# Lambda layer block on one core: the q parts are kept by chunk in DRAM and loaded in three pieces per chunk

## What is computed

```python
h = relu(bn(conv1x1(x, conv1_w)))                       # 512 -> 128 channels, x group-normed before
q = bn(conv1x1(h, q_w)); k = conv1x1(h, k_w); v = bn(conv1x1(h, v_w))   # 64, 16, 32 channels
pos = position_lambdas(emb, v)                          # 15x15 convolution, one per key
content_lambda = einsum('bkm,bvm->bkv', softmax(k), v)
out = einsum('bhkn,bkv->bhvn', q, content_lambda) + einsum('bhkn,bkvn->bhvn', q, pos)
h = bn(conv1x1(relu(bn(out)), conv3_w))                 # 128 -> 512
y = x + relu(h + residual)                              # residual: the group-normed x
```

## Time and profile before

| | us |
|---|---|
| median of 3 runs | 5737.59 |
| lowest and highest | 5727.03, 5744.17 |
| the profiled execution, its own time | 5744.49 |
| its span, first to last instruction | 5742.8 |
| PE busy in it | 4814.6 (84%) |
| DVE, ACT, POOL busy | 3049.6, 2281.4, 1042.7 |
| time of the DMA packets, share of 16 engines | 63.8% |

### The profile page before, as it was taken

How to read it: one execution, slowest core, us unless ns; L and a number is a source line. 1 busy time by engine, 2 the same in 40 slices (tenths; PEclk the granted TensorE clock), 3 DMA queues, 4 the chain that set the end, 5 groups by cost and what they waited for, 6 DMA issues and landing times.

```text
span 5742.8 us, 121523 instructions
## 1 busy us (share of the span) xinstructions
PE 4814.6 (84%) x49366; PEld 2811.5 (49%) x49366; DVE 3049.6 (53%) x4727; ACT 2281.4 (40%) x2753; POOL 1042.7 (18%) x561
## 2 busy tenths in 40 slices
PE   4888888888888888888888988888888888888887
PEld 2555455544455544554444545445554455454454
DVE  3456455565554554555555546545455454564554
ACT  1434344344343343443434433434434344343443
POOL 0012221112211122211222111221112221122212
PEclk8888889888998888998888988889988899888998
DMA  3567755667656677556675566765667755677556
GB/s 104 187 213 231 256 176 201 201 226 256 209 189 206 215 249 250 172 202 207 228 257 189 193 202 222 255 217 180 211 208 248 243 175 196 215 231 255 181 202 222
DMA packets 540275, 1217.58 MB, mean 212 GB/s; under 512 B 54312, under 2 KB 236588, under 8 KB 539820
## 3 DMA queue, kind: packets, MB, share of 16 engines
q1 hardware_dynamic: 539820, 1210.21, 63.8%
HBM read 777.68 MB, written 365.22 MB: 199 GB/s over the span
## 4 chain that ended last, share of the span: by engine, by line
PE 57%; SPq 11%; issue 10%; DVE 9%; DMA 8%; ACT 3%; POOL 1%; DVEq 0%; ACTq 0%; POOLq 0%
PE ring L524 16%; PE ring L505 13%; PE ring L649 11%; PE ring L580 6%; DMA q_parts<-region 6%; SPq L351 5%; PE ring L604 4%; DVE region L693 3%; PE ring L531 3%; DVE st L861 2%; SPq L358 2%; PE ring L536 2%; PE ring L614 2%; DMA Qt<-q_parts 1%; SPq L361 1%
## 5 line engine op out<-in xcount | busy, mean ns | idle before, releaser
L693 ACT COPY region<-ring 126x1024 f32<-126x1024 f32 x1024 | 1014.9, 1014 | 1660.8 <-PE ring L505 1645.8
L505 PE MATMUL ring<-Qt,Ep 96*126 96x256 bf16 x5120 | 862.7, 312 | 453.6 <-issue 293.7
L580 PE MATMUL ring<-h,w3T 128*128 128x512 f32 x2048 | 1067.8, 664 | 131.7 <-DVE S L1008 116.4
L693 DVE COPY region<-ring 126x1024 f32<-126x1024 f32 x512 | 623.6, 1218 | 939.7 <-PE ring L505 933.7
L524 PE MATMUL ring<-X,w1e 128*128 128x512 f32 x2048 | 971.3, 630 | 128.5 <-DVE w1e L885 128.5
L505 PEld LDWEIGHTS ring<-Qt,Ep 96*126 96x126 bf16 x5120 | 641.0, 154 | 743.7 <-issue 620.5
L1164 POOL TENSOR_TENSOR X<-X,S 128x1024 f32<-128x1024 f32 x320 | 750.3, 2349 | 1142.6 <-ACT S L732 1142.6
L649 PE MATMUL ring<-region,V 126*32 126x128 f32 x24576 | 872.1, 287 | 13.2 <-DVE region L693 12.8
L649 PEld LDWEIGHTS ring<-region,V 126*32 126x32 f32 x24576 | 667.1, 114 | 138.7 <-issue 129.4
L524 PEld LDWEIGHTS ring<-X,w1e 128*128 128x128 f32 x2048 | 408.0, 202 | 630.8 <-issue 627.5
L580 PEld LDWEIGHTS ring<-h,w3T 128*128 128x128 f32 x2048 | 407.4, 213 | 550.3 <-issue 376.7
(11 more groups left out here) (126 smaller groups left out, 3076.8 us busy)
## 6 DMA issues: line engine op xcount, KB each, us to landing
X<-x_dram SPq DMA_DIRECT2D x256, 2048.0 KB, 11.8
out_dram<-X SPq DMA_DIRECT2D x512, 512.0 KB, 6.7
Qt<-q_parts SPq DMA_DIRECT2D x768, 128.0 KB, 2.8
V<-v_windows SPq DMA_DIRECT2D x96, 1024.0 KB, 10.8
h<-S SPq DMA_DIRECT2D x1024, 64.0 KB, 2.0
q_parts<-region SPq DMA_DIRECT2D x128, 256.0 KB, 4.6
v_windows<-region SPq DMA_DIRECT2D x64, 512.0 KB, 6.2
V<-v_windows SPq DMA_DIRECT2D x32, 672.0 KB
```

The costliest lines, as they stand in the source:

```text
L505: last = nc.tensor.matmul(dst[0:TROWS, i * 256:(i + 1) * 256], taps(u, xo, yo), Q[:, :, xo * BLK + yo, :], start=(i % 2 == 0), stop=True, ...
L580: last = nc.tensor.matmul(dst[:, yb * HALF:(yb + 1) * HALF], w3T[:, t, :], src, start=True, stop=True)
L693: return engine_copy(dst, src)
```

## The change

The DRAM tensor is ordered by chunk: (chunk, part, key, head x pixel), so that a key's four heads of one chunk are one row of 8 KB. A store is now one DMA for each part: 64 partitions of 2 KB each into a target of 4 heads x 16 keys x 2 KB. A load is three DMAs, one for each part: part 0 is read three times over (a stride of 0 in front) into 48 partitions, part 1 twice into 32, part 2 once into 16, in rows of 8 KB. Partition g*16 + k of `Qt` now holds key k of product g, and its columns are ordered (chunk, head) instead of (head, chunk); the views of `Qt`, of the weights and the rest rows in `region` and of the setup's tables follow. The mask, which was written by two DMAs, takes six of 16 partitions.

```diff
-        qD = nc.dram_tensor("q_parts", (QC, NPART, N), BF16, kind="Internal").ap()
+        qD = nc.dram_tensor("q_parts", (NCH, NPART, DK, HEADS * CHUNK), BF16, kind="Internal").ap()
...
-        Qg = Qt[0:KG, :].rearrange("p (h c n b) -> p h c n b", h=HEADS, c=NCH, n=PIX)
+        Qg = Qt[0:KG, :].rearrange("p (c h n b) -> p c h n b", c=NCH, h=HEADS, n=PIX)
...
-        Wt = region[:, :].rearrange("p (u h b n) -> p u h b n", u=2, h=HEADS, b=64)
+        Wt = region[:, :].rearrange("p (u c h b n) -> p u c h b n", u=2, c=NCH, h=HEADS, b=16)
...
-                sp.dma_start(qD[:, 0, cols], q0[:, cols]).then_inc(q_out[j], 16)
-                sp.dma_start(qD[:, 1:NPART, cols], q12[:, :, cols]).then_inc(q_out[j], 16)
+                for a, src in ((0, q0[:, cols]), (1, q12[:, 0, cols]), (2, q12[:, 1, cols])):
+                    sp.dma_start(qD[j, a].rearrange("k (h n) -> h k n", h=HEADS), src).then_inc(q_out[j], 16)
 
             def load_q(im, j):
-                sp.wait_ge(q_out[j], im * 32 + 32)
-                for g, (a, _e) in enumerate(SPLIT):
-                    dst = bass.AP(Qt, g * (HEADS * N) + j * CHUNK, [[NG * HEADS * N, DK], [N, HEADS], [1, CHUNK]])
-                    sp.dma_start(dst, qD[:, a, j * CHUNK:(j + 1) * CHUNK].rearrange("(h k) n -> k h n", k=DK))\
-                        .then_inc(q_in[j], 16)
+
+                sp.wait_ge(q_out[j], im * 48 + 48)
+                n = HEADS * CHUNK
+                for a, g0, g1 in ((0, 0, 3), (1, 3, 5), (2, 5, 6)):
+                    src = bass.AP(qD.tensor, (j * NPART + a) * DK * n, [[0, g1 - g0], [n, DK], [1, n]])
+                    sp.dma_start(Qt[g0 * DK:g1 * DK, j * n:(j + 1) * n], src).then_inc(q_in[j], 16)
...
-            for i in range(2):
-                sp.dma_start(mask[:, i:i + 1], six[:, i, :]).then_inc(setup_mask, 16)
+            for g in range(NG):
+                sp.dma_start(mask[g * DK:(g + 1) * DK, :], six[:, g, :]).then_inc(setup_mask, 16)
...
-                        pe.wait_ge(q_in[j], im * (16 * NG) + 16 * NG)
+                        pe.wait_ge(q_in[j], im * (16 * NPART) + 16 * NPART)
...
-                                         Qg[:, :, c, half * 32:half * 32 + 32, 4 * k:4 * k + 4]
+                                         Qg[:, c, :, half * 32:half * 32 + 32, 4 * k:4 * k + 4]
```

More of the change, by code:

```diff
@@ L162, in lambda_block @@
         CLp = sb("CLp", [KG, DV], BF16)
-        qD = nc.dram_tensor("q_parts", (QC, NPART, N), BF16, kind="Internal").ap()
+        qD = nc.dram_tensor("q_parts", (NCH, NPART, DK, HEADS * CHUNK), BF16, kind="Internal").ap()
         vD = nc.dram_tensor("v_windows", (WPAD, WROWS, ROW), F32, kind="Internal").ap()
         vR = nc.dram_tensor("v_rest", (WPAD, ROW), F32, kind="Internal").ap()
-        Q = Qt[0:KG, :].rearrange("p (hc n b) -> p hc n b", hc=HEADS * NCH, n=PIX)
-        Qg = Qt[0:KG, :].rearrange("p (h c n b) -> p h c n b", h=HEADS, c=NCH, n=PIX)
+        Q = Qt[0:KG, :].rearrange("p (ch n b) -> p ch n b", ch=NCH * HEADS, n=PIX)
+        Qg = Qt[0:KG, :].rearrange("p (c h n b) -> p c h n b", c=NCH, h=HEADS, n=PIX)
         low = Qt[96:96 + WCOLS, :].bitcast(F32)
         Vrem = low[:, 0:NXB * ROW].rearrange("p (xb r) -> p xb r", xb=NXB)
-        Wrem = low[:, 2048:4096].rearrange("p (u h b n) -> p u h b n", u=2, h=HEADS, b=64)
+        Wrem = low[:, 2048:4096].rearrange("p (u c h b n) -> p u c h b n", u=2, c=NCH, h=HEADS, b=16)
         rep = low[0:DK, 4096:4096 + KG]
         clS = low[0:DK, 4096 + KG:4096 + KG + DV]
-        Wt = region[:, :].rearrange("p (u h b n) -> p u h b n", u=2, h=HEADS, b=64)
+        Wt = region[:, :].rearrange("p (u c h b n) -> p u c h b n", u=2, c=NCH, h=HEADS, b=16)
         T = S[:, :, :].rearrange("p h n -> p (h n)").rearrange("p (i n) -> p i n", i=2)
@@ L192, in lambda_block @@
         ident = region[:, o:o + P]; o += P
-        rep0 = region[0:DK, o:o + KG].rearrange("k (a g) -> k a g", g=NG); o += KG
-        six = region[0:DK, o:o + 2 * NG].rearrange("k (i g) -> k i g", g=NG); o += 2 * NG
+        rep0 = region[0:DK, o:o + KG].rearrange("k (g a) -> k g a", g=NG); o += KG
+        six = region[0:DK, o:o + 2 * NG].rearrange("k (g i) -> k g i", g=NG); o += 2 * NG
         RR = R * R
@@ L403, in _ @@
             sp.dma_start(wkvr[DV:KV, :], wk).then_inc(setup_in, 16)
-            emb_at = o - 2 * 128 - 2 * RR
             for g in range(NG):
-                dst = bass.AP(region, g * 16384 + emb_at, [[NG * 16384, DK], [1, RR]])
-                sp.dma_start(dst, emb.rearrange("k a b -> k (a b)")).then_inc(setup_in, 16)
+                sp.dma_start(emb6[g * DK:(g + 1) * DK, :], emb.rearrange("k a b -> k (a b)")).then_inc(setup_in, 16)
             sp.wait_ge(setup_pool, 1)
@@ L614, in rest @@
                         nc.tensor.matmul(dst.rearrange("p (h x y) -> p h x y", h=HEADS, x=4)[:, :, :, BLK - 1],
-                                         Vrem[:, xb, yb * DV:(yb + 1) * DV], Wrem[:, half, :, c * 16 + g, :],
+                                         Vrem[:, xb, yb * DV:(yb + 1) * DV], Wrem[:, half, c, :, g, :],
                                          start=False, stop=False, skip_group_check=True)
@@ L650, in lam @@
                                                         V[0:TROWS, VSLOT[t], xb, yb * DV:(yb + 1) * DV],
-                                                        Wt[0:TROWS, u % 2, :, c * 16 + g, :],
+                                                        Wt[0:TROWS, u % 2, c, :, g, :],
                                                         start=False, stop=(u % 3 == 2), skip_group_check=True)
@@ L691, in move_weights @@
             src = ring[at][0:TROWS, :].rearrange("p (n hb) -> p hb n", n=4)
-            dst = Wt[0:TROWS, u % 2, :, :, 4 * s:4 * s + 4].rearrange("p h b n -> p (h b) n")
+            dst = Wt[0:TROWS, u % 2, :, :, :, 4 * s:4 * s + 4].rearrange("p c h b n -> p (c h b) n")
             return engine_copy(dst, src)
@@ L696, in move_rest @@
             src = ring[at][96:96 + WCOLS, :].rearrange("p (n hb) -> p hb n", n=4)
-            return engine_copy(Wrem[:, half, :, :, :].rearrange("p h b n -> p (h b) n"), src)
+            return engine_copy(Wrem[:, half, :, :, :, :].rearrange("p c h b n -> p (c h b) n"), src)
         def move_sums(engine_copy, k):
@@ L1066, in _ @@
             dve.wait_ge(setup_pool, 5)
-            chain(nc.vector.tensor_copy(rep, rep0.rearrange("k a g -> k (a g)")))
-            dve.wait_ge(setup_mask, 32)
+            chain(nc.vector.tensor_copy(rep, rep0.rearrange("k g a -> k (g a)")))
+            dve.wait_ge(setup_mask, 16 * NG)
             chain(nc.vector.tensor_copy(ehi, emb6))
@@ L1126, in _ @@
                         pool.wait_ge(setup_gp, n)
-                        nc.gpsimd.memset(six[:, i, gg:gg + 1], -1.0).then_inc(setup_gp, 1)
+                        nc.gpsimd.memset(six[:, gg, i:i + 1], -1.0).then_inc(setup_gp, 1)
                         n += 1
@@ L1132, in _ @@
             nc.gpsimd.affine_select(out=rep0, in_=rep0, compare_op=ALU.not_equal, fill=1.0, base=0,
-                                    pattern=[[-1, DK], [0, NG]], channel_multiplier=1).then_inc(setup_gp, 1)
+                                    pattern=[[0, NG], [-1, DK]], channel_multiplier=1).then_inc(setup_gp, 1)
             nc.gpsimd.memset(grp[:, :], 1.0 / CPG).then_inc(setup_gp, 1)
```

## The result

| | us |
|---|---|
| before, median of 4 runs on the same chip | 5732.31 |
| changed, median of 4 runs | 7169.96 (7165.92 to 7184.53) |
| ratio | 1.2504, 95% interval 1.2482 to 1.2526 |
| forecast | 7081, range 6400 to 7750 |
| the changed kernel's profiled execution | 7171.97, span 7169.4 |

The change makes the kernel 25% slower. Between the two spans, 7169.4 and 5742.8, lie 1427 us, 44.6 us for each of the 32 images; forecast were 42.

The account below looks back on a forecast made before the run. The prediction took q's way through DRAM, set by SP's queue and the DMA engines, to bound the kernel; 32 images at 42 us more on 5744.5 gave 7088, corrected to 7081 us, range 6400 to 7750.

Parts of the forecast that it names:

- What bounds the kernel; a longer q way is paid in full, 32 times: q's way through DRAM sets the end; lengthening beyond the 3 us wait costs fully in each of 32 images.
- nothing in this stretch waits for PE: First q store to w0.0, 59.0 us: SP's queue and the DMA engines were said to set it.
- At most 3 us per image to win: PE's wait for q at the first weight tile, 96.9 us in 32 waits, was taken as the largest possible gain.
- The smaller outermost count decides: New q DMAs: the smaller outermost count of both sides sets the engines: 4 for stores, 3, 2 and 16 for loads.
- Rival 1: All 16 engines share every q transfer: at best 5641 us, or 5738 us; chance 0.12.
- 3- and 2-way loads on the same engines: Loads of parts 0 and 1: the 3 and the 2 engines were said to be the same lowest-numbered ones.
- The load's term, 10.4 us: Loads per chunk: 264 KB on the one engine serving every transfer, at 26 GB/s, take 10.4 us.
- rival 3: Two of the first load's three engines hinder each other at the target: 5 us more per chunk, 7722 us; chance 0.13.
- The store's term, 7.7 us instead of 1.9: Stores per chunk: 96 KB on each of 4 engines at 12.8 GB/s take 7.7 us.
- rival 2: As forecast, but stores reach 26 GB/s per engine: 6762 us; chance 0.2.
- The sum: First q store to w0.0: the busiest engine needs 102 us instead of 59.0, so 42 us more per image.
- Nothing for setup, for column orders, for the clock: Six mask DMAs, the new column order of Qt and weights, and PE's clock were each given zero.

Follow-up runs that it names:

- e8: Kernel before the change with SP's loads of q chunk 3 moved ahead of the v stores: 5635.97 us, ratio 0.9811.
- e9: e6 with e8's order, the loads of q chunk 3 ahead of the v stores: 5618.84 us, ratio 0.9767.
- e1: Changed kernel with partitions ordered (key, product), so its three loads have the 16 keys outermost; stores unchanged: 5851.62 us, ratio 1.0183.
- e3: e2 with the three loads of part 0 made one again (3 repeats outermost): 6734.74 us, ratio 1.1712.
- e4: e2 with the two loads of part 1 made one again (2 repeats outermost): 6557.61 us, ratio 1.1404.
- e7: Changed kernel with e6's eight stores by head; loads still with 3 and 2 repeats outermost: 6971.40 us, ratio 1.2138.
- e6: e1 with the stores cut by head into eight DMAs of 16 partitions per chunk: 5726.32 us, ratio 0.9971.
- e10: e4 with the 2-way load writing every second partition, 0 to 62, its engines 32 partitions apart: 6652.42 us, ratio 1.1575.
- e11: e4 with the 2-way load writing every second partition, 32 to 94, its engines in different halves: 6470.19 us, ratio 1.1258.
- e5: Changed kernel with six loads per chunk into every sixth partition, 8 KB rows, stores unchanged: 5962.27 us, ratio 1.0378.
- e2: Changed kernel with six loads of 16 neighbouring partitions per chunk, nothing repeated, stores unchanged: 5981.10 us, ratio 1.0401.

## Why the prediction was right, point by point

- *What bounds the kernel; a longer q way is paid in full, 32 times.* Shown for the path: 1468 us more wait, 1427 us more span; everything else on PE kept its time. But "nothing in this stretch waits for PE" was a misreading of the kernel before. In the chain of waits of that image, PE's work stands until chunk 2's store, by way of DVE, ACT and POOL, which make the parts of q:

```profile
2740.07 6.87 PE ring L524 x16
...
2752.91 2.14 POOL region L1157
...
2755.07 0.68 SPq L344
```

So the first half of the 59.0 us was set by the making of q, and a q way that gets a little longer is partly absorbed there. How much: the prediction's own sum for the kernel before, 4 x (1.9 + 1.7 + 3.8) with the reloads 10.1, outputs 4.6, v stores 7.0 and 1.2, gives 52.5 us of DMA work where 59.0 were measured, so some 6.5 us per image, an estimate.
- *At most 3 us per image to win.* Nearly: e8 wins 3.3 us and e9 4.1 ((5749 - 5619) / 32). The bound was the wait alone, and left out that PE runs at the low clock behind it, 1.2 us per image by e8; the prediction had allowed 0 to 1 us for the clock and taken zero.
- *The smaller outermost count decides.* Shown by the shares 0.26, 0.19, 0.12 and by e1, in which only the order of two steps of the same reading differs, and with it the order of the rows in the target: ratio 1.0183 instead of 1.2504. Rival 1 did not come.
- *3- and 2-way loads on the same engines.* Shown by e3 and e4, whose costs nearly add up; the single engine at 125.5 to 128 us fits it.
- *The load's term, 10.4 us.* Too small. It stood against 3.8 us of data before (768 KB at 208 GB/s), so it made 26 us per image of the sum; e7 against e6 gives 38.9. The term took 26 GB/s for one engine. The 25 GB/s measured at 125.5 to 128 us is the rate at the very end, behind the loads; from 109.5 to 128 us engine A carried its 264 and 96 KB, 369 thousand bytes, in 18.5 us, 20 GB/s on average. With the stores at the 23 GB/s that they reach alone (4.3 us), 14.2 us are left for the load, an estimate: 3.8 per chunk or 15 per image above the term. What slows the loads is open. That two of three engines get in each other's way was rival 3, at 5 us per chunk; e3 shows two engines 2.5 us late, and e10 against e11 shows 1.4 per chunk for another place in the target.
- *The store's term, 7.7 us instead of 1.9.* Too large: at 23 GB/s it is the 4.3 us, 3.4 less per chunk or 14 per image. The 12.8 GB/s per engine was taken from stores in which 16 engines share 64 partitions; four engines on them give 23 each. The nearest row by shape was the wrong one; rival 2 (26 GB/s) had the better rate. The kernels show less still, 3.8 us per image (e1 against e6) and 6.6 (the changed kernel against e7), where 4 x (4.3 - 1.9) would be 9.6; the time that is absorbed while q is being made fits the difference, and explains as well why e1 lay below its band.
- *The sum.* For load and store together it gave 18.1 us of engine A per chunk, against 18.5 in the quiet stretch, and for the whole way to w0.0 102 us, against 104.5 in the image read. It is this close by luck: the load was undersized by 15 us per image and the store oversized by 14. With 14.2 and 4.3 in their places, the same sum gives 103.7.
- *Nothing for setup, for column orders, for the clock.* The first q store is issued at 101.26 us against 101.75, so the setup cost nothing. PE's groups kept their times (L603 245.8 us in both kernels, L504 856.3 us against 862.7). The mean granted clock fell from 0.879 to 0.808, but PE's busy sum did not grow (4786.1 us against 4814.6), so the additional time at the low clock fell on idle time.
- *What would show it.* The wait was put at some 1400 us and is 1565. SP's own waits for "DMA q_parts<-region" grew from 310.0 to 703.7 us. Shares near 3/16 and 2/16 are there (0.19, 0.12), but with the next chunk's stores queued as well, so not in the pure form that was named. The page gives no time to landing for the new q transfers; in the chain of the image read the stores of chunks 1 to 3 land 14.5 to 17.6 us after their last issue, where "5 us or more" was named, and the last loads 15.8 us after theirs, above the 6 to 12 named for the first two.
- *Issuing on SP is worth nothing.* It fits the change, where SP waits for landings; with 16 engines it may be what e1 has over e5 (3.5 us per image).

## What to carry to other kernels

Before DMAs are merged into fewer and larger ones, look at the outermost count on both sides: a stride of 0 or a small dimension in front can hand a transfer to two or three engines. The DMA share in a quiet stretch tells the number of engines at once, and in e1 the same steps with the 16 keys in front gave the engines back. And ask what lies on the queue between a transfer that is waited for and its consumer: moving the four v stores behind the last q loads was worth 106 us, and the better shape of the transfer 16.

## What the hardware showed that was not expected

- One DMA engine carried 25 GB/s alone and 23 as one of four.
- SP was held while issuing: three stores, 1.8 us in quiet, took 10.51 and 13.45 us where the loads and an X reload were queued before them. Behind the loads alone, in the first image, they took 1.68 to 2.14 us. The v_windows stores took 11.65 us even there, against 3.72 before the change.
- The wait ahead of w0.0, 3.0 us per image, cost PE another 1.2 us per image at the low clock behind it (e8: output tiles of 644 instead of 664 ns).
- Loads into 16 neighbouring partitions kept all engines busy at 157 GB/s (e2), into every sixth partition half busy at 161 GB/s (e5), while issuing the latter took SP 0.62 us each instead of 0.49; the intervals of the two kernels' times overlap.
